# Self-attention of a fused decoder layer: GpSimd makes the centred, scaled rows a tile ahead and scales the weight pieces

## The reference

```python
x = x + attn(layernorm(x))            # self-attention, 16 heads of 16, BitNet-style linear layers
x = x + xattn(layernorm(x), ctx)      # cross-attention, 16 heads of 128, q and k rms-normed
x = x + ffn(layernorm(x))             # 8 experts, the best 2 for each token, 688 wide
```

```python
def bitlinear(x, w, g):
    x_norm = rmsnorm(x, g)
    x_q = activation_quant(x_norm)    # scale = 127 / max|row|; round; / scale
    w_q = weight_quant(w)             # scale = 1 / mean|w|; round and clip to -1..1; / scale
    return einsum('btc,oc->bto', x_q, w_q)
Q, K, V = bitlinear(x, wq, gq), bitlinear(x, wk, gk), bitlinear(x, wv, gv)
```

## Time and profile before

| | us |
|---|---|
| median of 3 runs (lowest, highest) | 864.79 (862.46, 867.49) |
| span of the profiled execution | 864.9 |
| TensorE busy over the span | 734.1 (85%) |
| VectorE | 572.7 (66%) |
| ScalarE | 456.5 (53%) |
| GpSimd | 376.6 (44%) |

### The profile page before, as it was taken

The page is one execution under the profiler, slowest core; times in us unless marked ns, Lnnn a source line. Parts: engine busy times, 40 slices in busy tenths (PEclk is TensorE's granted clock), DMA queues, the critical chain, the costliest instruction groups (busy, mean ns, idle before and its releaser), DMA issues. The chain is left out here.

```text
span 864.9 us, 26946 instructions
## 1 busy us (share of the span) xinstructions
PE 734.1 (85%) x10809; PEld 522.8 (60%) x10809; DVE 572.7 (66%) x1060; ACT 456.5 (53%) x875; POOL 376.6 (44%) x446
## 2 busy tenths in 40 slices
PE   0498888887886999999999995997299999999994
PEld 0387777775433565656566664766167776677772
DVE  5778788763886989899898996967843233233330
ACT  0578777654774666667566664534023333333331
POOL 0113222222254556556555556610136665555543
PEclk9999888876998999999999998999599999999998
DMA  9322232301564767566756663629848787788882
GB/s 322 109 55 52 52 63 64 87 22 30 156 193 150 178 131 182 135 177 160 185 131 165 168 167 110 210 59 421 317 95 146 141 141 141 139 139 138 141 129 38
DMA packets 192471, 121.91 MB, mean 141 GB/s; under 512 B 140800, under 2 KB 172800, under 8 KB 192224
## 3 DMA queue, kind: packets, MB, share of 16 engines
q1 hardware_dynamic: 178928, 103.54, 48.3%
q0 software_dynamic: 7488, 9.32, 6.6%
q10 hardware_dynamic: 5936, 7.34, 2.4%
HBM read 61.04 MB, written 27.00 MB: 102 GB/s over the span
## 5 line engine op out<-in xcount | busy, mean ns | idle before, releaser
L1749 DVE SCALAR_TENSOR_TENSOR f_slot_work<-psu,f_slot_work 128x688 f32<-128x688 f32 x39 | 34.1, 875 | 116.5 <-PE psu L1820 116.5
L1345 PE MATMUL xbank_a<-arena,x_o 128*128 128x256 f16 x768 | 97.0, 277 | 4.0 <-DVE x_o L1152 2.3
L1567 POOL DMA_INDIRECT out_dram<-f_y,f_to x39 | 62.2, 1596 | 80.1 <-ACT f_y L1625 63.9
L1345 PEld LDWEIGHTS xbank_a<-arena,x_o 128*128 128x128 f16 x768 | 73.5, 99 | 26.9 <-DVE x_o L1152 9.8
L1249 PE MATMUL xbank_qk<-arena 128*128 128x512 f16 x336 | 84.8, 390 | 5.0 <-PEq L188 4.7
L1837 PE MATMUL fbank<-arena,f_slot_work 128*128 (+1 forms) x663 | 82.8, 273 | 2.4 <-DMA f_slot_work<-hid_hl 2.4
L914 POOL TENSOR_SCALAR arena<-arena 128x512 f32<-128x512 f32 x25 | 37.2, 1489 | 92.6 <-DVE cT L1185 92.6
L1837 PEld LDWEIGHTS fbank<-arena,f_slot_work 128*128 128x128 f16 (+1 forms) x663 | 64.5, 98 | 20.8 <-issue 11.0
L1820 PE MATMUL psg<-wgu,f_slot_work 128*128 x468 | 75.0, 310 | 0.0
L1820 PE MATMUL psu<-wgu,f_slot_work 128*128 x468 | 74.6, 309 | 0.0
L1617 ACT CAST hid_hl<-f_slot_work 128x688 f16<-128x688 f32 x39 | 29.9, 767 | 77.3 <-DVE f_slot_work L1749 67.4
(11 more groups left out here) (285 smaller groups left out, 1708.3 us busy)
## 6 DMA issues: line engine op xcount, KB each, us to landing
arena<-in_wx SPq DMA_DIRECT2D x51, 256.0 KB, 3.0
wgu<-w_hl SPq DMA_DIRECT2D x2, 5504.0 KB, 25.6
ao<-key_norms SPq DMA_DIRECT2D x64, 128.0 KB, 3.3
w_hl<-cT SPq DMA_DIRECT2D x26, 256.0 KB, 2.1
w_hl<-x_pair SPq DMA_DIRECT2D x25, 256.0 KB, 2.2
ao<-in_wx SPq DMA_DIRECT2D x10, 256.0 KB, 3.1
w_hl<-ao SPq DMA_DIRECT2D x10, 256.0 KB, 2.1
x_sb<-in_x SPq DMA_DIRECT2D x4, 512.0 KB, 9.6
```

Source lines behind the costliest of these rows:

```text
L1345: last = nc.tensor.matmul(acc[t // 2][:, (t % 2) * C:(t % 2 + 1) * C], o_hl[h % 2][:, a, at:at + P], wvo[:, b, e, :], start=(e == 0 and j ...
L1567: nc.gpsimd.indirect_dma_start(out=dram["out_rows"], out_offset=bass.IndirectOffsetOnAxis(ap=to[n % 2][:, 0:1], axis=0), in_=y[n % 2][:, : ...
L1749: nc.vector.scalar_tensor_tensor(out=h3, in0=psu[:, :].rearrange("p (c n) -> p c n", c=2)[:, :, 0:FH], scalar=HID_UP / (H_UP * W_UP), in1= ...
```

## The change

The row-wise product u moves from VectorE to GpSimd and is made one tile ahead, in two buffers. The second buffer is the memory of the raw weights. GpSimd makes it in two instructions: `xc`, the centred row, and u, its product with the three gain rows. The scaling of the raw pieces (L353) moves from ScalarE to GpSimd, into `split_low`. Two unused columns of the constants now hold the factors.

```diff
-        u = sb("u", [P, QKV, C], F32)
+        u = [sb("u", [P, QKV, C], F32), w_raw[:, 0:QKV, :]]
+        xc = sb("xc", [P, C], F32)
...
+                def spread(i):
+                    if i == 0:
+                        pool.wait_ge(stats_ready, 1)
+                        pool.wait_ge(in_g, 64)
+                    need(pool, u_done, i)
+                    nc.gpsimd.tensor_tensor(xc[:, :], x_sb[:, i, :], mv[:, i, 0:1].to_broadcast([P, C]), ALU.subtract).then_inc(xc_done, 1)
+                    pool.wait_ge(xc_done, i + 1)
+                    need(pool, z_done, i - 1)
+                    if i == 1:
+                        pool.wait_ge(w_ready, 2 * NCH + 1)
+                    nc.gpsimd.tensor_tensor(u[i % 2][:, :, :], xc[:, :].unsqueeze(1).to_broadcast([P, QKV, C]), gains[:, 0:QKV, :], ALU.mult).then_inc(u_done, 1)
...
                 def split_low(n, behind):
-                    pool.wait_ge(up_done, n + 1)
+                    pool.wait_ge(high_done, n + 1)
                     if tile(behind):
                         pool.wait_ge(sc_done, 2 * behind + 2)
-                    parts = splits[n][4]
-                    nc.gpsimd.tensor_tensor(splits[n][2], raw[n % 2][...], splits[n][1], ALU.subtract).then_inc(low_done, 1)
-
+                    src, high, low, up, parts = splits[n]
+                    factor = cst[:, CONSTS + 3:CONSTS + 4] if up == W_UP else cst[:, CONSTS + 4:CONSTS + 5]
+                    nc.gpsimd.tensor_tensor(raw[n % 2][:, :], raw[n % 2][:, :], factor.to_broadcast([P, SPLIT]), ALU.mult).then_inc(up_done, 1)
+                    pool.wait_ge(up_done, n + 1)
+                    nc.gpsimd.tensor_tensor(low, raw[n % 2][...], high, ALU.subtract).then_inc(low_done, 1)
+
+                spread(0)
                 for t in steps:
                     if pair(t, 2) is not None:
                         gained(pair(t, 2))
                     if pair(t, 7) is not None:
                         h_low(pair(t, 7))
+                    if tile(t + 5):
+                        spread(t + 5)
                     if tile(t + 4):
                         key_scale(t + 4)
                     if t % 2 and 0 <= (t + 3) // 2 < NSPLIT:
                         split_low((t + 3) // 2, t + 5)
...
                     nc.scalar.mul(high, part, up).then_inc(high_done, 1)
-                    nc.scalar.mul(part, part, up).then_inc(up_done, 1)
...
                 def front(i):
-                    need(dve, z_done, i)
-                    nc.vector.scalar_tensor_tensor(out=u[:, :, :], in0=x_sb[:, i, :].unsqueeze(1).to_broadcast([P, QKV, C]), scalar=mv[:, i, 0:1],
-                                                   in1=gains[:, 0:QKV, :], op0=ALU.subtract, op1=ALU.mult).then_inc(u_done, 1)
                     dve.wait_ge(u_done, i + 1)
-                    c.link(nc.vector.tensor_reduce(amax[:, i, :], u[:, :, :], AX.X, ALU.max, apply_absolute_value=True))
+                    c.link(nc.vector.tensor_reduce(amax[:, i, :], u[i % 2][:, :, :], AX.X, ALU.max, apply_absolute_value=True))
```

More of the change, by code:

```diff
@@ L155, in attention @@
         zT_in, zoT_in, hT_in = [sem(f"a_zT_in{i}") for i in range(2)], sem("a_zoT_in"), sem("a_hT_in")
-        u_done, sc_done, yq_done, z_done, kd_done, t_done, zT_done = (sem("a_" + n) for n in ("u_done", "sc_done", "yq_done", "z_done", "kd_done", "t_done", "zT_done"))
+        xc_done, u_done, sc_done, yq_done, z_done, kd_done, t_done, zT_done = (sem("a_" + n) for n in ("xc_done", "u_done", "sc_done", "yq_done", "z_done", "kd_done", "t_done", "zT_done"))
         q_done, k_done, v_done, qf_done, kf_done, vb_done = (sem("a_" + n) for n in ("q_done", "k_done", "v_done", "qf_done", "kf_done", "vb_done"))
@@ L252, in split_low @@
                 def split_low(n, behind):
-                    pool.wait_ge(up_done, n + 1)
+                    pool.wait_ge(high_done, n + 1)
                     if tile(behind):
                         pool.wait_ge(sc_done, 2 * behind + 2)
-                    parts = splits[n][4]
-                    nc.gpsimd.tensor_tensor(splits[n][2], raw[n % 2][:, :].rearrange("p (a n) -> p a n", a=parts) if parts > 1 else raw[n % 2][:, :], splits[n][1], ALU.subtract).then_inc(low_done, 1)
+                    src, high, low, up, parts = splits[n]
+                    factor = cst[:, CONSTS + 3:CONSTS + 4] if up == W_UP else cst[:, CONSTS + 4:CONSTS + 5]
+                    nc.gpsimd.tensor_tensor(raw[n % 2][:, :], raw[n % 2][:, :], factor.to_broadcast([P, SPLIT]), ALU.mult).then_inc(up_done, 1)
+                    pool.wait_ge(up_done, n + 1)
+                    nc.gpsimd.tensor_tensor(low, raw[n % 2][:, :].rearrange("p (a n) -> p a n", a=parts) if parts > 1 else raw[n % 2][:, :], high, ALU.subtract).then_inc(low_done, 1)
+                spread(0)
                 for t in steps:
@@ L296, in quantise @@
                     for j in range(QKV):
-                        nc.scalar.activation(u[:, j, :], u[:, j, :], ACT.Identity, scale=qsc[:, i, j:j + 1], bias=magic).then_inc(yq_done, 1)
+                        nc.scalar.activation(u[i % 2][:, j, :], u[i % 2][:, j, :], ACT.Identity, scale=qsc[:, i, j:j + 1], bias=magic).then_inc(yq_done, 1)
                 def key_scales(i):
@@ L437, in integers @@
                         dve.wait_ge(zT_in[i % 2], 16 * (i // 2))
-                    nc.vector.tensor_scalar(z[i % 2][:, :], u[:, :, :].rearrange("p j c -> p (j c)"), MAGIC, None, ALU.subtract).then_inc(z_done, 1)
+                    nc.vector.tensor_scalar(z[i % 2][:, :], u[i % 2][:, :, :].rearrange("p j c -> p (j c)"), MAGIC, None, ALU.subtract).then_inc(z_done, 1)
                 def keys(i):
@@ L1855, in constants @@
     c = np.concatenate([np.asarray(x, np.float32) for x in parts], axis=1)
-    values = np.tile(np.array([LN_EPS, 1e-6, -MAGIC, 0, 0, MAGIC, np.log(H_UP), 0], np.float32), (P, 1))
+    values = np.tile(np.array([LN_EPS, 1e-6, -MAGIC, W_UP, CTX_UP, MAGIC, np.log(H_UP), 0], np.float32), (P, 1))
     numbers = np.tile(np.concatenate([np.arange(NE), np.arange(NSLOT)]).astype(np.float32), (P, 1))
```

## The result

The changed kernel takes 871.84 us (median of 5 runs, 866.74 to 875.21) against 866.65 us (862.46 to 875.59) for the kernel before in the same comparison: ratio 1.0081, 95% interval 1.0045 to 1.0116. So it is slower by 4 to 7 us. The forecast was 863.8 us and a range of 856 to 870: the first measurement lies 1.8 us above that range, the repetition (869.92) just inside it. Ratios leave out the slow executions, those over 1.5% above the fastest of their kernel (one each in e3, e10 and e12, two in e15), while medians and ranges are of all. One correction of what stands above: by its span of 864.9 us, the profiled execution of before is not one of the three runs named there but that of 866.65 us, since every run takes 1.8 us more than its span. For the changed kernel it is 875.21 and 873.4.

A forecast was written before the change was run, and what follows sets the result against it. No engine was full; ScalarE's path set even steps, VectorE or TensorE's scores odd ones. Early lateness of +2.8 us, later gains and +1.1 at the end summed to -1.0 us: 863.8 us, range 856 to 870.

The forecast's parts named there:

- The order on its queue: GpSimd in odd steps: weight product, low part, gain row, subtraction, u product; u ready 6.6 to 8.2 us after the scales.
- ScalarE's 0.94 us in an even step: Even steps of self-attention: removing ScalarE's second weight scaling shortens the path to the probabilities' copy by 0.94 us.
- The price of the last piece: End of self-attention: a 2.1 us GpSimd product replaces 1.05 us of ScalarE, +1.1 us with nothing to hide it.
- step -1: +2.8: Early odd step (t = -1): u comes after the 2.7 us pitch, so the reduction starts about 2.8 us late.
- steps 7, 9 and 11: Late odd steps: the small L432 held behind GpSimd's low half, losing 0.6 to 0.7 of 1.05 us won.
- The start. I book 0: First tile: VectorE and GpSimd may block each other, up to 2 us, won back by step -2; 0, between -2 and +2.
- step 3: Odd step (t = 3): pitch 5.9 us is short again, the front waits for u, lateness +2.4 us.
- the sum: Lateness added over self-attention's steps: +2.8 in step -1, falling to -0.2 by step 11, -1.0 us at the end.
- The price of z: Steps 6, 8 and 10: VectorE's z held about 1.3 us by GpSimd's u product, partly hidden by a 0.40 us wait.
- Rival 2: GpSimd's queue sets the pace from even steps' scales to the next front, where chain exceeds 8.6 us: 869 to 871, chance 0.23.
- rival 1: Throughout self-attention, collisions and queue cost little: about 12 us faster, 853, or half of it, 858; chance 0.24.
- Rival 3: TensorE's clock decides: one half-speed spell, about 5 us, less gives 859, one more 869; chance 0.08, split evenly.

The follow-up runs named there:

- e3: Changed kernel with u of tile 3 made a step earlier, ahead of the first weight piece: 863.41 us, 1.0003 of the kernel before.
- e10: Changed kernel with u of tile 3 earlier, u product in three parts, and ScalarE scaling the last weight piece: 859.06 us, 0.9944 of the kernel before.
- e12: Changed kernel, but each u product on GpSimd waits until VectorE has finished the previous tile's front: 866.38 us, 1.0019 of the kernel before.
- e15: Changed kernel with u of tile 3 a step earlier and u products waiting for the front before: 861.69 us, 0.9939 of the kernel before.
- e7: The changed kernel run again without edits: 869.92 us, 1.0046 of the kernel before.
- e16: Repeat of the kernel before with only the weight scaling moved to GpSimd, except the last piece: 856.75 us, 0.9907 of the kernel before.
- e1: Kernel before with only the weight scaling moved to GpSimd, u staying on VectorE: 857.61 us, 0.9926 of the kernel before.
- e8: Kernel before with the weight scaling moved to GpSimd except the last piece, u staying on VectorE: 857.81 us, 0.9897 of the kernel before.
- e5: Kernel before with 20 idle matmuls in TensorE's gaps at the start: 861.46 us, 0.9962 of the kernel before.
- e6: Changed kernel with 20 idle matmuls in TensorE's gaps at the start: 869.38 us, 1.0041 of the kernel before.
- e4: Changed kernel with GpSimd's 768-wide u product cut into three of 256: 862.02 us, 0.9979 of the kernel before.
- e14: Kernel before with three extra VectorE reductions in the front of step -1: 871.07 us, 1.0068 of the kernel before.
- e9: Changed kernel with u of tile 3 made before the first weight piece and the u product in three parts: 859.32 us, 0.9960 of the kernel before.
- e13: Kernel before with six extra VectorE reductions in the front of step -1: 873.78 us, 1.0110 of the kernel before.

## Why the prediction was wrong

**Right.** The sizes on GpSimd: 0.61, 1.81 and 1.89 us where 0.70, 1.65 and 2.10 were taken, 57.9 against 59 us in all. The order on its queue. Which instructions are held (z, and the small ones behind the low half). ScalarE's 0.94 us in an even step: the gap of the earlier trace rows shrank by 0.96, in e7 and in e16. The price of the last piece: +1.0 us by e1's trace, +1.1 booked, and e8 against e1 gives 0.3% (2.5 us), by medians not apart from nothing. And the delay of the front in step -1 by the queue alone: 2.9 us in e12 against 2.8.

**Wrong: the term "step -1: +2.8" leaves out the holds of the small instructions, which the prediction put at nothing everywhere but in steps 7, 9 and 11.** The maximum of step -1 is 5.6 to 5.8 us late. That is 2.9 us of the queue, which e12 shows alone, and L447 held for 1.5 us in step -3 and again in step -1, by the product that GpSimd makes for the tile *after* the one VectorE is at. I had asked what stands in front of u in GpSimd's queue, and not what GpSimd does once it has delivered it. The booking "The start. I book 0" fails by the first of these holds and not by its own reason: GpSimd's work makes the first front 0.8 to 1.0 us late, and in e12, where only the hold is gone, this is won back by step -2 as the prediction had it (the front is 0.25 us early); in the changed kernel that front is 0.9 to 1.1 us late. The earlier trace rows had already shown the 128x2 instruction held, so "no row shows it" was too quick. In steps 7 and 9 the holds are 1.0 us (L445 held to 1.02 us for 0.23, L447 0.43 for 0.19) against 0.6 to 0.7 booked.

**Wrong too: the second such place, step 3.** By e7's trace, lateness ran 5.8, 5.8, 5.8, 5.4, 7.7, 8.3, 7.6, 6.6, 6.1, 5.0, 5.1, 4.1 us in steps -1 to 10, where the sum had 2.8, 2.8, 2.8, 2.0, 2.4, 1.5, 1.1, 0.5, 0.1 and from step 8 -0.2 (its own terms give -0.3 there): 3.0 us above at the start, 5.3 above in step 3, where L447 is held once more (1.69 us) behind a front that waited 2.06 us. Up to step 10 the distance stays between 4.3 and 6.8, so that the won-back part comes as the sum has it, from the wrong height. Then it is 6.4 and 7.0 us late in steps 11 and 12, 1.2 in steps 13 and 14, and 0.3 at the end of the stage, where the sum had -1.0. The fall of 5.8 us is the shorter half-speed spell described under e7, for which the sum had 0.9. So this one execution comes out near the sum by a second error of the opposite sign; that is luck, and the medians, 869.92 and 871.84, don't have it in full.

The Trainium skill, page "SBUF — State Buffer", section "Who interferes with whom", says that a VectorE instruction with two SBUF inputs waits for the end of a GpSimd instruction that reads SBUF and was issued first. L447 ending 0.02 us after the product agrees, and a rule of which I had used one case should have been asked of every small instruction of the front.

**The price of z** is not settled. It was held in one profile of the changed kernel and not in the other, which has 0.53 to 0.68 us. The prediction called itself wrong if z stayed near 0.53 us throughout; e7's execution does nearly that, and it is one of the faster ones of its kernel. So how often z is held, and what part of the medians it makes, is open. Fronts wait for u in steps -1 and 3 only, as forecast.

**The rivals.** Rival 2 is nearest by its time (869 to 871) and its sign, and its words "decides where chain exceeds pitch" hold; its place is wrong. The chain exceeds the pitch of 2.7 and 5.9 us in steps -1 and 3, and not that of 8.6 from step 7 on, where the fronts of e7 come no later from pair to pair. Of rival 1's saving of 12 us, 5 are there once the start is mended (e15, 0.9939), with collisions still in the trace. Rival 3, the clock, moves single executions (225.56 against 212.31 us for the end of the stage in two profiles of one kernel) and gives or takes 5 us in step 12, about what the rival had as its price; whether it also has a part in the medians of the changed kernel is open, since e5 and e6 failed to hold it equal.

**What is shown.** By medians: removing the wait in step -1 (e3) wins back about 4 to 7 us, shortening the holds (e4) 6 to 9, wait and hold together (e15) about 9 to 12. Removing the hold alone (e12) gives about 2 to 5, of which the lower is not clear of noise. (All four are differences of ratios to 1.0081 and 1.0046, mostly from other sets of runs.) By traces: what makes up the lateness in step -1, that a 2.9 us delay put into the old kernel at that place stays whole to the end of the stage (e14), and, with the spell of step 12 allowed for, that e3's stage is about 5 us shorter than e7's. Not shown: e12's gain in its trace, whose stage ends 0.5 us after e7's with the same short spell; how often each length of the spell occurs, and so what it does to the medians; why the gains overlap (e9); and why the medians of e13 and e14 rise by 3 to 4 us more than their delay.

The version to keep is e8's: ScalarE's scaling moves to GpSimd except for the last piece, and u stays on VectorE: 0.9897 and 0.9907 in two sets.

## What to carry to other kernels

In this kernel, work moved "a tile ahead" onto an in-order queue was ahead only where the queue in front of it was shorter than the consumer's pitch (6.9 us from the scales to the front in e12, against pitches of 2.7, 5.9 and 8.6). So look at the steps of the start, where pitches are shortest, since a delay there was not absorbed (e14). Beside every small instruction of the receiving engine, ask what the helper engine is doing at that moment, its *next* item too. And choose what to move by the path and not by the busy sum: ScalarE's scaling (10 us busy, ahead of TensorE's longest wait) gained, VectorE's u (16 us busy) lost. Lastly, compare two traces step by step past the place that you explain: here a change of clock in step 12 was larger than most of the terms.

## What the runs showed of the hardware

- A VectorE instruction of 0.19 us (128x3, two SBUF inputs) took 1.68 to 1.71 us beside a 1.81 us GpSimd product, a 128x3 floor of 0.23 us took up to 1.81 beside such a product (e7, step 5), and a 0.53 us z 1.94. A reciprocal between them stayed at 0.18 us. The small ones end with GpSimd's instruction, z 0.4 us after it.
- Cutting that product in three cost GpSimd 0.6 us (2.41 against 1.81) and brought the holds behind it down to 0.65 us and z to about 0.9: VectorE got in between the parts.
- The first recorded full-speed spell of TensorE began at 58.7 and at 74.4 us in two executions of one kernel.
- TensorE's half-speed spell in step 12 lasted 13.7 us in six of the 18 profiles (before, e3, e6, e13, e14, e15) and 3.4 us in the others.
